# Graph attention on one Trainium2 core: ScalarE scales the heads, the bias moves to the wide product, whose opening is written out anew

## What is computed

```python
def gat_conv(x, src, dst, W, a_src, a_dst, b):
    h = (x @ W).reshape(N, H, C)                      # N 1250, H 4 heads, C 192
    as_n = (h * a_src).sum(-1)
    ad_n = (h * a_dst).sum(-1)
    e = jax.nn.leaky_relu(as_n[src] + ad_n[dst], NEG_SLOPE)
    m = jax.ops.segment_max(e, dst, num_segments=N)
    p = jnp.exp(e - m[dst])
    s = jax.ops.segment_sum(p, dst, num_segments=N)
    alpha = p / (s[dst] + 1e-16)
    out = jax.ops.segment_sum(alpha[:, :, None] * h[src], dst, num_segments=N)
    return out.reshape(N, H * C) + b
...
xs = [jax.nn.relu(gat_conv(x1, src, dst, W, a_s, a_d, b)) for W, a_s, a_d, b in (...)]
node_emb = jnp.concatenate(xs, axis=1)
return jax.nn.relu(node_emb @ W_out + b_out)
```

## Time and profile before

| | us |
|---|---|
| median of 3 runs (3175.09 to 3182.57) | 3178.88 |
| the profiled execution | 3182.64 |
| its span | 3180.9 |
| PE busy (82%) | 2602.6 |
| DVE busy (63%) | 2000.4 |
| ACT busy (43%) | 1356.1 |

### The profile page before, as it was taken

How to read it: one execution, slowest core, us unless ns; L and a number is a source line. 1 busy time by engine, 2 the same in 40 slices (tenths; PEclk the granted TensorE clock), 3 DMA queues, 4 the chain that set the end, 5 groups by cost and what they waited for, 6 DMA issues and landing times. The chain is left out here.

```text
span 3180.9 us, 40026 instructions
## 1 busy us (share of the span) xinstructions
PE 2602.6 (82%) x14620; PEld 2308.1 (73%) x14621; DVE 2000.4 (63%) x2885; ACT 1356.1 (43%) x2206; POOL 358.5 (11%) x309
## 2 busy tenths in 40 slices
PE   5774878887986968984899779869897998999876
PEld 5663778887886868982788738457666776999766
DVE  7886278877967962225655444452796555899654
ACT  0343267575665641111566410031697102777430
POOL 1351030040031000000223201000000000111000
PEclk9996989998998979996999969979998997999978
DMA  0113101112111134211899770114552222443304
GB/s 33 25 39 85 48 23 44 50 44 66 41 52 38 57 108 102 48 35 43 281 245 249 197 155 0 49 72 148 147 122 51 60 86 49 98 102 86 92 1 102
DMA packets 107496, 268.23 MB, mean 84 GB/s; under 512 B 10934, under 2 KB 49320, under 8 KB 106346
## 3 DMA queue, kind: packets, MB, share of 16 engines
q1 hardware_dynamic: 99730, 239.43, 27.6%
q0 software_dynamic: 7616, 26.74, 3.9%
HBM read 195.58 MB, written 66.73 MB: 82 GB/s over the span
## 5 line engine op out<-in xcount | busy, mean ns | idle before, releaser
L888 PE MATMUL ps<-h,e_gat_aggregate 125*125 125x193 f32 x2400 | 408.9, 334 | 79.4 <-DVE e_gat_aggregate L872 63.3
L888 PEld LDWEIGHTS ps<-h,e_gat_aggregate 125*125 125x125 f32 x2400 | 402.3, 192 | 85.9 <-DVE e_gat_aggregate L872 66.8
L833 ACT ACTIVATE e_gat_aggregate<-row_gat_aggregate,from_src 125x1250 f32<-125x1250 f32 x120 | 160.7, 1339 | 155.7 <-PE ps L888 131.0
L870 DVE TENSOR_TENSOR e_gat_aggregate<-e_gat_aggregate 125x1250 f32<-125x1250 f32 x120 | 175.1, 1460 | 76.9 <-ACT e_gat_aggregate L836 76.9
L103 PE MATMUL ps<-gat_w_pair_gat_scores,x_turned 128*125 128x384 f32 x1080 | 196.3, 345 | 33.0 <-DVE gat_w_pair_gat_scores L748 33.0
L103 PEld LDWEIGHTS ps<-gat_w_pair_gat_scores,x_turned 128*125 128x125 f32 x1080 | 195.2, 191 | 33.9 <-DVE gat_w_pair_gat_scores L748 33.8
L103 PE MATMUL ps<-w_pair_dense_rows_from,col_dense_rows_from 128*125 128x384 f32 x1080 | 206.0, 349 | 1.8 <-DVE col_dense_rows_from L1024 1.8
L2366 DVE TENSOR_TENSOR ln_home<-p_attend,p_high_attend 125x1254 fp32r<-125x1254 f32 x120 | 184.4, 1550 | 27.9 <-ACT p_high_attend L2352 25.2
L103 PEld LDWEIGHTS ps<-w_pair_dense_rows_from,col_dense_rows_from 128*125 128x125 f32 x1080 | 195.1, 193 | 2.5 <-DVE col_dense_rows_from L1024 2.5
L2344 ACT ACTIVATE p_attend<-ps 125x1254 f32<-125x1254 f32 (+2 forms) x168 | 148.6, 915 | 80.2 <-PE ps L2307 79.3
L1859 DVE TENSOR_SCALAR_CACHE_REDUCE res_attention_statistics<-ps 125x1250 f32<-125x1250 f32 x120 | 173.1, 1459 | 11.4 <-PE ps L1836 5.1
(11 more groups left out here) (384 smaller groups left out, 5170.5 us busy)
## 6 DMA issues: line engine op xcount, KB each, us to landing
stock<-in_moe_w SPq DMA_DIRECT2D x34, 1152.0 KB
row_gat_aggregate<-r_scratch SPq DMA_DIRECT2D x24, 625.0 KB, 6.3
V_home<-q_scratch SPq DMA_DIRECT2D x44, 312.5 KB, 6.3
ln_home<-q_scratch SPq DMA_DIRECT2D x36, 312.5 KB
ln_home<-k_scratch SPq DMA_DIRECT2D x36, 312.5 KB
stock<-in_gat_w SPq DMA_DIRECT2D x4, 2304.0 KB, 8.8
rows_dense_rows_from<-node_scratch SPq DMA_DIRECT2D x8, 1080.0 KB
q_scratch<-V_home SPq DMA_DIRECT2D x6, 1250.0 KB, 4.5
```

What stands on the lines that cost most here:

```text
L833: a.activation(e[:, n % 3, 0, :], row[0:TP, head % 2, 0, :], ACT.Exp, bias=from_src[:, head, t:t + 1])
L870: v.tensor_tensor(e[:, n % 3, 0, :], e[:, n % 3, 0, :], e[:, n % 3, 1, :], ALU.max).then_inc(p_step, 1)
L888: last = pe.matmul(ps[0:TP, bank(head, d // 2), d % 2 * (C + 1):(d % 2 + 1) * (C + 1)], e[:, n % 3, 0, d * TP:(d + 1) * TP], h[:, t, head, :],
```

## The change

In `gat_aggregate` VectorE keeps the row sums and reciprocals (`inverse`, behind the next head's first tile). The scaling goes to ScalarE (`leave`), between the exponentials of the next head's tiles 1 to 4; of the last head ScalarE scales six tiles and VectorE four. Bias and ReLU are no longer applied there: the wide product adds the bias of the three layers to the turned groups in PSUM (`move`), ScalarE applies ReLU with its high part and VectorE with its low part. Turns use four banks and not two. The third layer is written out behind a loop of two rounds; in it `stock` takes only four weights of `W_out` and, in the place of the other two, the 1536 old columns of tile 0. In the wide product the order of turns, splits and products of the first two tiles is written out.

```diff
 
             sp.wait_ge(w_split, KD)
-            load_ahead(sp, g, [(i["gat_w"][bass.ds(layer * D + D, D), :], 0)], ahead_in)
+            load_ahead(sp, g, [(i["gat_w"][bass.ds(layer * D + D, following * 128), :], 0)], ahead_in)
             sp.wait_ge(r_out, 1)
...
+def gat_aggregate(nc, g, layer, i, r_scratch, node_scratch, first_rows=None):
...
-            sp.dma_start(bias[:], i["gat_b"][bass.ds(layer, 1), :].partition_broadcast(128)).then_inc(bias_in, 16)
+            if first_rows:
+                move_rows(sp, first_rows[0], node_scratch[0:TP, 0:OLD], first_rows[1])
...
-                    sp.wait_ge(node_ready, 2 * head + part + 1)
+                    if head == HEADS - 1 and part == 1:
+                        sp.wait_ge(last_read, 2)
+                    else:
+                        sp.wait_ge(bank_read, HEAD_BANKS * head + 3 + 2 * part)
...
+        def leave(eng, head, tiles, done):
+
+            for t in tiles:
+                if t in (0, 6) and head >= 1:
+                    eng.wait_ge(node_stored[t // 6], 32 * head)
+                sums = ps[0:TP, bank(head, t // 2), t % 2 * (C + 1):t % 2 * (C + 1) + C]
+                if eng is nc.scalar:
+                    last = eng.activation(node[:, t, :], sums, ACT.Copy, scale=rsum[:, 1, t:t + 1])
+                else:
+                    last = eng.tensor_scalar(node[:, t, :], sums, rsum[:, 1, t:t + 1], None, ALU.mult)
+                if t % 2:
+                    last.then_inc(done, 1)
...
+                    if head >= 1 and t in (1, 2, 3, 4):
+                        if t == 1:
+                            a.wait_ge(inverse_ready, head)
+                        leave(a, head - 1, range(0, 4) if t == 1 else range(2 * t, 2 * t + 2), bank_read)
+            a.wait_ge(inverse_ready, HEADS)
+            leave(a, HEADS - 1, range(0, 6), bank_read)
...
+            def inverse(head):
+
+                if head >= 1:
+                    v.wait_ge(bank_read, HEAD_BANKS * head)
...
-                step(v.reciprocal(rsum[:, 1, :], rsum[:, 0, :]))
-                for t in range(NT):
-                    if t in (0, 6) and head >= 1:
-                        v.wait_ge(node_stored[t // 6], 32 * head)
-                    last = v.scalar_tensor_tensor(node[:, t, :], ps[0:TP, bank(head, t // 2), t % 2 * (C + 1):t % 2 * (C + 1) + C],
-                                                  rsum[:, 1, t:t + 1], bias[0:TP, head * C:(head + 1) * C], ALU.mult, ALU.add)
-                    if t % 2:
-                        last.then_inc(bank_read, 1)
-                    if t in (5, NT - 1):
-                        tiles = slice(0, 6) if t == 5 else slice(6, NT)
-                        v.wait_ge(bank_read, HEAD_BANKS * head + (t + 1) // 2)
-                        v.tensor_scalar(node[:, tiles], node[:, tiles], 0.0, None, ALU.max).then_inc(node_ready, 1)
+                v.reciprocal(rsum[:, 1, :], rsum[:, 0, :]).then_inc(inverse_ready, 1)
...
-                    if t == 1 and head >= 1:
-                        leave(head - 1)
-            leave(HEADS - 1)
+                    if t == 0 and head >= 1:
+                        inverse(head - 1)
+            inverse(HEADS - 1)
+            v.wait_ge(inverse_ready, HEADS)
+            leave(v, HEADS - 1, range(6, NT), last_read)
 
         @block.tensor
...
+    TURN_BANKS = (0, 1, 6, 7)
...
+            def load_weights(k):
+                sp.dma_start(w[:, k % KD, :], weight[k * 128:(k + 1) * 128, :]).then_inc(w_in[k % KD], 16)
+
+            sp.dma_start(shift[:], source_bias).then_inc(shift_in, 16)
+            move_rows(sp, second[:, 0:OLD], source[TP:2 * TP, 0:OLD], second_in[0])
+            for part in range(2):
+                sp.wait_ge(node_stored[part], 32 * HEADS)
+            move_rows(sp, rows[:, OLD:kt * 128], source[0:TP, OLD:kt * 128], first_in)
+            move_rows(sp, second[:, OLD:kt * 128], source[TP:2 * TP, OLD:kt * 128], second_in[1])
+            sp.wait_ge(turned, OLD // 512)
+            for k in range(KEPT, KD):
+                load_weights(k)
             for k in range(KD, kt):
                 sp.wait_ge(w_split, k - KD + 1)
...
+                load_weights(k)
             sp.dma_start(b[:], bias.partition_broadcast(128)).then_inc(bias_in, 16)
...
+            move_rows(sp, x, x_in.rearrange("(t p) d -> p t d", p=TP), x_loaded)
+            for t in range(2, NT):
+                sp.wait_ge(turned, groups * t)
+                move_rows(sp, rows, source[t * TP:(t + 1) * TP, :], row_in)
...
+                if n >= 4:
+                    pe.wait_ge(col_ready, n - 3)
...
+            def opening(t, k):
+                pe.wait_ge(col_ready, t * groups + k // 4 + 1)
                 pe.wait_ge(w_split, k + 1)
-                products(0, k)
-                products(1, k)
+                products(t, k)
+
+            for q in range(3):
+                turn(0, q)
+            opening(0, 0)
+            opening(0, 1)
+            turn(0, 3)
+            opening(0, 2)
+            turn(0, 4)
+            opening(0, 3)
+            turn(1, 0)
+            turn(1, 1)
+            opening(0, 4)
+            turn(1, 2)
+            opening(0, 5)
+            turn(1, 3)
+            turn(1, 4)
+            for k in range(KD):
+                opening(1, k)
+            for k in range(KD, kt):
+                opening(0, k)
+                opening(1, k)
...
+            def high(t, *qs):
+                for q in qs:
+                    group, ks = turned_group(t, q)
+                    a.wait_ge(shifted, t * groups + q + 1)
+                    a.activation(col[:, t % 2, 0, ks, :], group, ACT.Relu).then_inc(col_high, 1)
+
+            high(0, 0, 1, 2)
+            weights(0, 1, 2)
+            high(0, 3)
+            weights(3)
+            high(0, 4)
+            high(1, 0)
+            weights(4)
+            high(1, 1)
+            weights(5)
+            high(1, 2, 3, 4)
+            weights(*range(KD, kt))
+            for t in range(2, NT):
+                a.wait_ge(summed, t - 1)
+                high(t, *range(groups))
...
+            def move(t, q):
+                group, ks = turned_group(t, q)
+                v.wait_ge(turned, t * groups + q + 1)
+                v.tensor_tensor(group, group, shift[:, ks].unsqueeze(2).broadcast_to([128, ks.stop - ks.start, TP]),
+                                ALU.add).then_inc(shifted, 1)
+
+            def low(t, q):
+                group, ks = turned_group(t, q)
+                v.wait_ge(col_high, t * groups + q + 1)
+                v.scalar_tensor_tensor(col[:, t % 2, 1, ks, :], group, 0.0, col[:, t % 2, 0, ks, :].bitcast(F32),
+                                       ALU.max, ALU.subtract).then_inc(col_ready, 1)
+
+            def weights(*ks):
+                for k in ks:
+                    v.wait_ge(w_high, k + 1)
+                    v.tensor_tensor(w_pair[:, 1, k, :], w[:, k % KD, :], w_pair[:, 0, k, :].bitcast(F32), ALU.subtract).then_inc(w_split, 1)
+
+            v.wait_ge(shift_in, 16)
+            move(0, 0)
+            move(0, 1)
+            low(0, 0)
+            move(0, 2)
+            low(0, 1)
+            weights(0)
+            low(0, 2)
+            weights(1)
+            move(0, 3)
+            weights(2)
+            low(0, 3)
+            move(0, 4)
+            weights(3)
+            low(0, 4)
+            move(1, 0)
+            move(1, 1)
+            low(1, 0)
+            weights(4)
+            low(1, 1)
+            move(1, 2)
+            weights(5)
+            low(1, 2)
+            move(1, 3)
+            move(1, 4)
+            low(1, 3)
+            low(1, 4)
+            weights(*range(KD, kt))
             v.wait_ge(bias_in, 16)
...
+            v.wait_ge(x_loaded, 32)
             for t in range(NT):
                 if 2 <= t + 1 < NT:
...
+                    move(t + 1, 0)
+                    for q in range(groups):
+                        if q + 1 < groups:
+                            move(t + 1, q + 1)
+                        low(t + 1, q)
...
-            with nc.Fori(0, 3) as layer:
+            with nc.Fori(0, 2) as layer:
                 gat_scores(nc, g, layer, i, r_scratch)
                 gat_aggregate(nc, g, layer, i, r_scratch, node_scratch)
+            gat_scores(nc, g, 2, i, r_scratch, following=KEPT)
+            gat_aggregate(nc, g, 2, i, r_scratch, node_scratch, first_rows=(stock(g, KEPT * D, 1, OLD)[0:TP, 0], g["old_in"]))
```

133 lines of the change are left out of this document (36 added, 97 removed).

## The result

The changed kernel takes 3156.52 us (median of 5 runs, 3149.85 to 3159.83), the kernel before 3179.07 beside it (5 runs). The ratio is 0.9921, 95% interval 0.9906 to 0.9935: 25.1 us less by the ratio, with 20.7 to 29.9 in the interval. The forecast was 31 less. One later execution of the changed kernel took 3290.44 us at a granted clock of 0.79 where the others have 0.90; it is left out of every comparison here. The profiled execution has a span of 3154.8 us, before 3180.9.

The account below looks back on a forecast made before the run. TensorE was taken as the engine nearly always busy in aggregations, with time lost at seams and the wide product's opening. 28.9 + 5.4 + 1.3 - 4.5 = 31.1 us less, from the median 3178.9 to 3148; range 3137 to 3164.

Parts of the forecast that it names:

- seams: Passages between heads in the aggregations: scaling on ScalarE was to save 3.2 us each, 28.9 for nine.
- tails of three layers: From a layer's last matmul to its last store issue: 1.8 us less a layer, 5.4 in all.
- third layer without a table load: Start of the third layer, written out: ScalarE needs no table load, 1.3 us saved once.
- the wide product's opening and its tiles: First tiles of the wide product: tile 2's rows 5.7 us late, 1.2 given back, 4.5 more; later tiles nothing.
- The price of a scaling: In the seam: 0.32 us for each 192-wide scaling on ScalarE, bounds 0.25 and 0.57.
- 1.15 instead of 4.3: Cost of a seam in us after and before the change, from which 3.2 saved was taken.
- all four issues, no longer held between, end at 895.4: Tail of a layer: first store at 892.9, SyncE's four issues done at 895.4, 1.8 us less a layer.
- Of the code that now stands twice I see no price: Third layer written out behind the loop: the doubled code was to cost no more than +-1 us.
- Opening pays: Rival, wide product's opening: matmul at full clock and tile 2's rows on time, -4 not +4.5, about 3139; chance 0.16.
- ScalarE is no new bound: Rival, at the seam: ScalarE becomes the bound at 0.5 us a scaling or more, half saved, 3162; chance 0.14.
- No table load came between exponentials and scalings: Rival, seams: table loads at each change add 10.3 us a seam on ScalarE, about 3240; chance 0.03.
- The seam did not keep a wait of the old size: Rival: seams keep another wait of the same size, time within 0.2% (about 6 us); chance 0.04.

Follow-up runs that it names:

- x among the weights: Changed kernel with x's ten tiles loaded two behind each of weights 6 to 10, instead of behind weight 17 and the bias: 3141.63 us, ratio 0.9883.
- the old order: Changed kernel with the wide product's first two tiles as before (ten turns, six weight splits, then all products): 3146.29 us, ratio 0.9899.
- the three added edits: Changed kernel with x's tiles loaded among the weights, no loop around the layers and two buffers for rows: together 3116.64 us, ratio 0.9812.

## Why the prediction was right, and where it was off

In the profiles of before and after, by stretch:

| us less | forecast | in the rows |
|---|---|---|
| seams | 28.9 | 31.7 |
| tails of three layers | 5.4 | 2.7 |
| third layer without a table load | 1.3 | 1.5 |
| layer 2, ScalarE late where the loop turns | 0 | -2.2 |
| the wide product's opening and its tiles | -4.5 | -4.4 |
| sum | 31.1 | 29.3 |

The two profiles differ by 26.1 us, the runs by 25.1. The first aggregation and its first heads came 4.6 us later in the changed kernel's profile, which is spread, and stretches that the change leaves alone took 1.4 less. The signs and the mechanisms were right. That the sum came within 2 us of the rows is in part luck: the seams were put 2.8 too low, and the tails and the loop 4.9 too high.

- **The seams, 28.9 forecast, 31.7 in the rows.** The mechanism was right: both waits on banks are gone, two short ones on e are left. The price of a scaling was right (0.32 by the line; four in 1.36, two in 0.75). Two things were mis-sized. The first is the subtraction "1.15 instead of 4.3" (which gives 28.4 for nine, not 28.9): 4.3 is the time beyond ten tiles, of which only 3.80 were waits, while 1.15 was a sum of waits alone. Waits against waits, 3.80 less 0.80 is 3.00, which is what an ordinary seam gave (2.94, so 26.5). The second was put at nothing: in one head of each layer the waits were followed by 3.4 us at half the clock, 1.7 us a layer, 5.1 in all, and that went with the waits. The granted clock of 0.97 in the earlier trace rows was its trace. The edit that put the work back on VectorE splits an ordinary seam: 1.39 for bias and ReLU, 1.55 for the engine, and with the wide product undisturbed the latter came back in the time as 13.7.
- **The tails, 5.4 forecast, 2.7 in the rows** (0.82, 0.89 and 1.04 from the last row sums to the next phase). The step that failed is "all four issues, no longer held between, end at 895.4". The first store did go 0.9 us earlier. But four unheld issues take 3.5 us, since the later ones grow to 1.16 and 1.48. Nor does ScalarE's share matter there: with VectorE alone the tail is 7.89 against 7.82. The gain is the bias and the ReLU.
- **The third layer written out, 1.3 forecast.** The load is gone and 1.5 us with it. "Of the code that now stands twice I see no price" did not hold for the loop that stayed: at its turn ScalarE starts 2.5 us behind the phase and 2.2 us are lost. Both conditions were varied: without the loop, or with the scalings off ScalarE, the late start is gone. The cause behind it stays open.
- **The opening, +4.5 forecast, +4.4 in the rows.** Tile 2's turn was forecast for r = 71.3 and came at 71.4, released by a DMA, TensorE idle for 10.46 us before it (7 forecast, since its products ended at r = 61.0 and not 64). TensorE had its full clock from r = 12.5 on, but for a dip at 1152 to 1156, while the forecast had it at half clock until r = 31.8; it made no difference, because the queue sets the end. That was shown from both sides: x among the weights removed the wait and 12.4 us, the old order moved the weights 8 us forward and gave 7.3.
- **The rivals.** "Opening pays" fell here, and would have come true with one more edit: with x out of the way, the mixed order is the earlier one in the profile. ScalarE is no new bound: TensorE waits for e at two tiles, and not behind them. No table load came between exponentials and scalings. The seam did not keep a wait of the old size.

The Trainium skill ("ScalarE: Activation LUTs", Rules for kernel authors) wants multiplications on VectorE. The runs disagree for this place: the same ten scalings there cost 13.7 us more over nine seams, though one of them is a little shorter on VectorE (411 against 435 ns).

## What to carry to other kernels

What counts is which engine is awaited, and not which one does the work quicker. Subtract like from like: waits from waits, never a sum of waits from an excess over the pace. When waits go, look at the granted clock behind them too. Before an opening is reordered for TensorE, look at what the last asked-for load has behind it in the same queue; here x, not needed until the sums, stood in front of rows that were. A short wait that recurs behind each tile can be worth more than its length (here 19.7 us for 12.0), and a second buffer for it gave the most of the three added edits. And where code is added to an engine inside a loop, compare that engine's first instruction behind the turn of the loop.

## What the hardware showed that was not expected

- A wait of 2.44 us for rows was followed by 3.4 us at a granted clock of 0.5, and by 18 products in 4.78 us instead of 3.40. Six such waits, 12.0 us in all, cost 19.7. In the kernel before, waits of 1.79 and 2.02 us in a seam did the same once in each layer, for 1.7 us each.
- With ScalarE's scalings in the loop, its first instruction behind the turn of the loop came 2.37 to 2.53 us behind the phase in six profiles; with the loop but without them it came at 0.10, and without the loop at 0.02 or less.
- Four DMA issues in a row on SyncE took 0.33, 0.42, 1.16 and 1.48 us with nothing between them, so an earlier start bought no earlier end beyond its own 0.9.
- Ten loads of x's tiles among the weights, 20 issues of 0.3 to 0.4 us each, did not delay the weights' last issue (r = 38.7 against 37.4) enough to move the products' end (r = 61.2 in both).
- One kernel, profiled twice, reached its first aggregation 4.5 us apart (479.29 and 483.81).
